# Adding products of zeros on TensorE to the edge passes of a graph network kernel

## What is computed

```
x = x + L0(relu(ln(x)))    # msg = relu(h[src] + edge_attr_16 @ We + be), summed by dst, then an MLP
x = x + L1(relu(ln(x)))    # ten steps of h = 0.9 * A h + 0.1 * h0, A the normalised adjacency matrix
x = x + L2(relu(ln(x)))    # three attention layers:
    # hx = h @ W_node; ef = relu(edge_attr_3 @ W_e1 + b_e1) @ W_e2 + b_e2
    # a = sigmoid(relu([hx[dst], hx[src], edge_attr_3] @ Wa1 + ba1) @ Wa2 + ba2)
    # out = segment_sum(a * (hx[src] + ef), dst) + bias; layer norm; relu (not in the third); + h
x = x + L3(relu(ln(x)))    # silu(bn([h[dst'], h[src'] - h[dst']] @ W.T)), summed by the first end of the edge
```

## Time and profile before

| | us |
|---|---|
| median of three runs | 5724.86 (5715.06 to 5729.33) |
| the profiled execution | 5753.65 |
| its span, first to last instruction | 5751.8 |
| granted TensorE clock, mean over the span | 0.775 |

### The profile page before, as it was taken

The page is one execution under the profiler, slowest core; times in us unless marked ns, Lnnn a source line. Parts: engine busy times, 40 slices in busy tenths (PEclk is TensorE's granted clock), DMA queues, the critical chain, the costliest instruction groups (busy, mean ns, idle before and its releaser), DMA issues.

```text
span 5751.8 us, 80895 instructions
## 1 busy us (share of the span) xinstructions
PE 3486.7 (61%) x20001; PEld 2461.0 (43%) x20012; DVE 2848.6 (50%) x10579; ACT 927.6 (16%) x3266; POOL 3031.5 (53%) x3058
## 2 busy tenths in 40 slices
PE   2550077777789999856666555666566666444444
PEld 1430034444333443345555445555455555333333
DVE  7840078777641111255555645555555555533333
ACT  0000023333210000011111111111111111111111
POOL 3787655544488882045555255555345555355454
PEclk9999988889879999967677667777677777555555
DMA  4311122223379999711111211111211112111111
GB/s 136 82 24 9 48 64 68 69 70 70 62 268 338 358 354 350 269 48 41 42 42 42 38 40 42 43 42 42 40 40 42 42 43 42 18 19 19 18 19 21
DMA packets 293596, 498.22 MB, mean 87 GB/s; under 512 B 169174, under 2 KB 207203, under 8 KB 291962
## 3 DMA queue, kind: packets, MB, share of 16 engines
q1 hardware_dynamic: 118407, 339.94, 16.7%
q0 software_dynamic: 92160, 115.72, 11.0%
q10 hardware_dynamic: 82800, 40.01, 2.4%
HBM read 435.57 MB, written 58.97 MB: 86 GB/s over the span
## 4 chain that ended last, share of the span: by engine, by line
PE 38%; another core or an unknown queue 22%; DVE 14%; issue 12%; POOL 8%; ACT 2%; DVEq 1%; DMA 1%; SPq 0%; ACTq 0%; POOLq 0%
PE ps L1495 34%; POOL rows_dst L755 8%; DVE arena L1096 3%; DVE arena L1095 2%; PE ps L1721 1%; DVE arena L1078 1%; PE ps L1598 1%; DVE arena L1114 1%; DVE arena L1112 1%; DVE arena L1110 1%; DMA arena<-in_edge_attr_dram 1%; PE ps L1673 1%; ACT arena L1461 1%; DVE arena L1268 1%
## 5 line engine op out<-in xcount | busy, mean ns | idle before, releaser
L770 POOL DMA_INDIRECT arena<-table,arena x2080 | 2036.6, 979 | 2368.2 <-DMA arena<-rows_dst 1463.4
L1495 PE MATMUL ps<-arena 128*128 128x96 f32 (+3 forms) x9176 | 1652.6, 357 | 608.8 <-issue 199.6
L1495 PEld LDWEIGHTS ps<-arena 128*128 128x128 f32 (+3 forms) x9176 | 1169.9, 209 | 1004.0 <-issue 694.1
L1598 PE MATMUL ps<-ident,arena 128*96 128x128 f32 x416 | 152.0, 365 | 1183.1 <-ACT arena L1461 631.7
L1095 DVE TENSOR_SCALAR arena<-iota_row_b,arena 128x128 bf16<-128x128 bf16 x1664 | 437.0, 263 | 681.7 <-remote 528.1
L1495 PE MATMUL ps<-arena,nodes 125*64 125x500 f32 (+2 forms) x3144 | 654.6, 538 | 27.7 <-DVEq L1187 16.5
L1598 PEld LDWEIGHTS ps<-ident,arena 128*96 128x96 f32 x416 | 66.3, 159 | 1252.9 <-ACT arena L1461 633.8
L755 POOL DMA_INDIRECT rows_dst<-stage,arena x400 | 483.1, 1208 | 197.1 <-issue 121.6
L1108 DVE TENSOR_TENSOR arena<-ps,arena 128x256 f32<-128x256 f32 x416 | 175.4, 422 | 819.8 <-remote 634.4
L1096 DVE TENSOR_SCALAR arena<-iota_row_b,arena 128x128 f32<-128x128 bf16 x2080 | 580.5, 295 | 0.0
L728 POOL DMA_INDIRECT rows_src<-stage,stage_at x400 | 483.3, 1208 | 119.1 <-issue 116.3
(11 more groups left out here) (283 smaller groups left out, 3812.9 us busy)
## 6 DMA issues: line engine op xcount, KB each, us to landing
arena<-dense SPq DMA_DIRECT2D x240, 750.0 KB
nodes<-dense SPq DMA_DIRECT2D x60, 750.0 KB
dense<-arena ACTq DMA_DIRECT2D x150, 250.0 KB
arena<-table,arena POOLq DMA_INDIRECT x2080
arena<-dense SPq DMA_DIRECT2D x60, 500.0 KB
arena<-rows_dst SPq DMA_DIRECT2D x208, 96.0 KB
arena<-dense SPq DMA_DIRECT2D x6, 2000.0 KB
arena<-pair_rows SPq DMA_DIRECT2D x12, 976.6 KB
```

The source lines that it names most:

```text
L770: nc.gpsimd.indirect_dma_start(rows[:, u, k, 0:width], None, frm, bass.IndirectOffsetOnAxis(ap=p[:, c, j, c_other:c_other + 1].bitcast(I32 ...
L1495: return nc.tensor.matmul(to, lhsT, rhs, start=start, stop=stop, skip_group_check=True)
L1598: nc.tensor.transpose(to, pay[:, c, j:j + K, :].rearrange("p k c -> p (k c)"), ident[:]).then_inc(tr_ready, 1)
```

## The change

`add_zeros(count)` issues `count` matmuls of a 128x128 block of zeros by 128x512 zeros, in bf16, with `start` and `stop` off: each adds zero to every value of PSUM bank 3, the last bank of the sums. They wait for no semaphore and increment none. TensorE runs its matmuls in order.

In an attention layer a turn gets seven behind the one-hots' transposition (in all but the last turn) and seven behind `sum_up`. In the last pass it is eleven and eleven. The other engines' instructions are the same.

```diff
+            def add_zeros(count):
+
+                for _ in range(count):
+                    mm(ps[:, FB, :], zeros_b[:, 0:128], zeros_b[:], start=False, stop=False)
+
...
                     if more:
                         hidden(u + 1)
+                        add_zeros(7)
                     if before == 2:
                         sum_up(i, m, u - 2, 1)
+                    add_zeros(7)
                 over_units(pe, turn2)
...
                 if more:
                     turn_one_hots(m, u + 1)
+                    add_zeros(11)
                 if before == 2:
                     sum_up(i, m, u - 2, 0)
+                add_zeros(11)
             over_units(pe, turn3)
```

## The result

The changed kernel takes 5938.74 us (median of 4 runs, 5926.84 to 5954.33) against 5727.09 for the kernel before: a ratio of 1.0375, with a 95% interval of 1.0344 to 1.0407. It is slower by 212 us; 860 were forecast. The direction was right, the size was not.

The account below looks back on a forecast made before the run. It took a loop of loads, eight gathers and late-seen TensorE increments as the bound. Attention +806 and free turns +54, last pass 0, made 5753.65 + 860 = 6614, less 29 for the median: 6585 us; range 5540 to 6820.

Parts of the forecast that it names:

- What bounds the kernel: Layers and last pass: a loop of load, eight gathers and late answer sets the pace, 14.78 and 14.64 us a chunk.
- the hold: TensorE's increments, once gathers have flown 3 to 4 us, are seen only about 2.7 us after the last gather.
- The price of a product: On TensorE: 0.21 us each at the high clock, 0.43 at the low; seven take 1.5 or 3.0 us.
- The turn: TensorE's turn in a layer, with fourteen products at the high clock: 3.66 + 2.98 = 6.64 us.
- The even unit's transposition: In a layer's chunk, it starts 7.9 us after the load, 5.2 after the first gather, where answers come late.
- the payload copy comes at s + 2.77 + 8.85 + 2.79 = s + 14.4: In the layers, ScalarE's copy for the even unit waits until 2.79 us behind the last gather; s is the load.
- Copy to next load: In the layers, from payload copy to next load: 6.4 + 0.1 us, near the low clock, giving s + 20.9.
- Free turns: Some six turns a layer, outside the held chunks, go at TensorE's pace, 3.0 us longer each: +54 us.
- Last pass: Two turns of 6.7 us with products fit into 14.1 a chunk; taken as 0, bounds -60 to +110 us.
- Fits in the idle time: Rival: both turns of 6.64 us fit into the layers' 14.78 a chunk; only +54, 5779 us; chance 0.13.
- Faster: the hold goes with the idling: Rival: a busy TensorE ends the late answers, turns set the pace at 13.28 us a chunk; 5523 us; chance 0.22.
- Turns that outlast the gathers: Rival: clock stays low, so turns of 11.7 us in layers and 13.8 in last pass; 7550 us; chance 0.03.

Follow-up runs that it names:

- paced: Kernel before, with GpSimd waiting in layers and last pass until each unit's four gathers have landed: 5687.48 us against 5718.04, ratio 0.9946.
- layers_only: Changed kernel without the last pass's products: 4852.51 us against 4592.08 for the kernel before, ratio 1.0566.
- four_a: Kernel before, with different product trials in the three layers and a wait behind each unit's first gather in the last pass: 5000.87 us against 4588.24.
- staggered: Kernel before, with GpSimd waiting behind a unit's second gather for the four of the unit before: 4589.51 us, ratio 1.0011.
- paused: Kernel before, with GpSimd clearing a scratch tile three times, each with a drain, after every four gathers: 5880.76 us, ratio 1.2821.

## Why the prediction was wrong in size

- **What bounds the kernel: right for the chip measured on, and shown.** The loop of load, eight gathers and a delayed answer was the pace there. Take the delay away, by the pacing or by the chip, and the waits of unknown release go to 1% or 0%; on the chips without it the kernel before runs at 10.0 us a chunk, the eight gathers alone. The forecast took the hold for a property of the kernel; it goes with the chip too. Its cause is not shown.
- **The price of a product: right.** Seven took 1.67 us with the tail, 1.5 and 0.2 forecast.
- **The turn: 5.92 us where nothing in it waits, not 6.64.** The turn of 3.66 holds waits for ScalarE and VectorE, which the products fill (2709.95 to 2715.87, and again on the other chip). Adding 2.98 to it counted that time twice.
- **The even unit's transposition comes when gathers are under way: right.** 7.4 us after the load, 7.9 forecast; the half microsecond is mostly the shorter turn.
- **The step that failed: "the payload copy comes at s + 2.77 + 8.85 + 2.79 = s + 14.4".** It comes at s + 10.4, and 3.5 of the 4.0 us between are the wait: 3.0 us where 6.5 were forecast (the other 0.5 is the earlier transposition). The mechanism was taken too broadly. Not every increment made 3 to 4 us into a run of gathers waits until 2.7 us behind the last gather: in the changed kernel the first late one leaves some 3 us after it was made, mostly ahead of the last gather, and those made after it wait to the end. The payload's was the first in line. The rows from which the forecast took its 2.7 us were of later ones. In the chunk of the earlier trace rows the records show the one-hots' increment, made at 2555.57, 4.9 us after the first gather, come through at 2558.57, ahead of the last gather; the second transposition, made 8.6 us after the first gather, stood two places behind it. The hidden product of the earlier trace rows had another increment waiting before it, made at 3510.16 and recorded at 3517.24. I carried that length over to an increment made 5.2 us after it. The trace of before has 18 payload transpositions made 4 to 5 us after a first gather; they were copied 1.5 us later on average, 5.15 at most, and none of them was among my rows. They would have set the term, or at least its lower bound. This step is 4.0 x 141, some 560 us, of the excess.
- **Copy to next load: 5.5 us, not 6.5.** The forecast has 6.4 and 0.1. No run shows the 6.4 (the work behind the copy adds up to 4.2 + 3.0 = 7.2 at the low clock); what the changed kernel shows in its place is 5.49 in all. The clock stayed at 0.92 on average and not at the low level: with a wait of 3 us in place of 6.5 TensorE idled less. 1.0 x 141 is some 140 more. Taking 20.5 rather than 20.9 takes 56 off; 20.9 - 4.0 - 1.0 = 15.9, as measured.
- **Free turns: +54 forecast.** The layers grew by 61, 57 and 65, of which 57, 52 and 58 are the 47 chunks: about 16 in all.
- **Last pass: right on that chip**, 772 against 773, for the reason given: two turns fit into the 14.1. Where gathers alone set the pace they do not fit, and it costs 118.
- **The rivals.** "Fits in the idle time" needed an undelayed transposition: refuted by the 3.01. "Faster: the hold goes with the idling": refuted, since TensorE at 0.92 was delayed as before; the clock came back and the last pass, at 0.97, gained one microsecond. What the Trainium skill advises (TensorE: Matmul & The Clock Gate, section "Why this matters for your kernels"), a TensorE without gaps, gave the clock here and not the time. Turns that outlast the gathers, the mechanism on the other chips, was priced only at the low clock, as a mishap.
- The forecast without its failed and mis-sized terms, 860 - 560 - 140 + 56 - 38, is 178. The four stages grew by 182; the two profiled runs are 173 apart and the medians 212, since the profiled run of before lies 27 us above its median and that of the changed kernel 12 below.

No version beats both kernels everywhere: paced is 0.5% faster with the delay, which is little, and without it such a wait, run with the products in, makes a chunk 14.6 us instead of 10.0.

## What to carry over

Where answers come at once, added work on an engine costs nothing until its turn outlasts the pace of the loop, and then the whole excess: compare the two paces, and not busy shares. Where they do not, that is not enough: on the first chip two turns are 11.84 us and the loop had 14.78, and the products still cost 1.2 us a chunk, because they moved one answered step to where its answer came late. A pace that rests on waits without a recorded releaser may belong to the chip: measure the kernel before on a second chip ahead of pricing anything by it. And do not carry the length of a wait from one place in a round to another where the trace has no row.

## What the runs showed that was not expected

- One program, two kinds of chips: 5727 and 4585 us, a difference of 1142 us, with gathers of much the same 977 to 988 ns. In the first pass too, the 48 loads take 811.8 us (750.3 to 1562.1) on the one and 659.5 (737.5 to 1397.0) on the other.
- A copy that waits for a transposition begins 0.31 to 0.54 us after it in all units of the layers in layers_only, gathers or not. Where increments are delayed, it takes up to 6.3 us in the changed kernel while gathers go out.
- Four gathers have landed some 3 us after the issue of the fourth began. The gather that waits for them starts 3.4 us after it in paced and 3.2 in four_a's last pass (medians), and hardly one is held up in staggered, where it would start 3.75 after it anyway. In four_a's last pass GpSimd idles 0.88 us ahead of such a gather, 0.30 ahead of the others:
```profile
4701.31 0.95 POOL L771 DMA_INDIRECT arena<-table,arena  x1 [0.88 <-DMA arena<-table,arena]
```
- Four gathers, a clearing of 0.28 us and a drain leave GpSimd idle for 1.55 us (paused), where it is idle 0.30 between two gathers.
